# High parts of queries and keys written twice to DRAM in stack order, in a windowed attention and recurrent-gate kernel on one Trainium2 core

## What is computed

```
qkv = x @ w_in.T                       # 16 heads of 16 features
scores = q k^T / 4 + slope_h * distance, in blocks of 128 queries against their own and the previous block
o = softmax(scores) v ;  x1 = layernorm(x + o @ w_out.T)
for t in 16 "time steps" (the first axis of x1), batch 512:
    f, i = sigmoid(x1_t Wf + c Uf + bf), sigmoid(x1_t Wi + c Ui + bi);  g = tanh(x1_t Wc + c Uc + bc)
    c = f * c + i * g
h = tanh(x1 Wo + c_final Uo + bo) ;  out = layernorm(x1 + h)
```

## Time and profile before

| | |
|---|---|
| median of three runs | 1033.92 us (1031.19 to 1034.87) |
| the profiled execution | 1031.44 us, its span 1029.7 us |
| TensorE, VectorE, ScalarE busy | 914.9, 768.7, 547.5 us |
| moved by DMA | 131.98 MB, 125 GB/s of HBM traffic over the span |
| written to HBM | 50.33 MB |
| the first raw scores start at | 42.47 us |
| time of one pass in the steady part | 51.7 to 51.9 us (first raw scores of successive sequences) |

### The profile page before, as it was taken

How to read it: one execution, slowest core, us unless ns; L and a number is a source line. 1 busy time by engine, 2 the same in 40 slices (tenths; PEclk the granted TensorE clock), 3 DMA queues, 4 the chain that set the end, 5 groups by cost and what they waited for, 6 DMA issues and landing times.

```text
span 1029.7 us, 25853 instructions
## 1 busy us (share of the span) xinstructions
PE 914.9 (89%) x9500; PEld 750.3 (73%) x9500; DVE 768.7 (75%) x2882; ACT 547.5 (53%) x1101; POOL 376.7 (37%) x621
## 2 busy tenths in 40 slices
PE   3287879999999999999999999999999989889994
PEld 2164667878787878787878787878787867678884
DVE  6356767787879797979797979797979684336885
ACT  5034544555555555656565656565555544325876
POOL 3023433343434344444444444444434342201443
PEclk9578989999999999999999999999999989999998
DMA  7545353545353535353535453545354410112764
GB/s 199 143 134 140 106 166 110 155 125 151 113 156 117 151 111 156 107 157 118 152 111 151 123 148 115 153 119 150 118 131 120 125 50 23 42 53 71 215 201 137
DMA packets 92957, 131.98 MB, mean 128 GB/s; under 512 B 12008, under 2 KB 46696, under 8 KB 92832
## 3 DMA queue, kind: packets, MB, share of 16 engines
q1 hardware_dynamic: 92832, 130.34, 43.9%
HBM read 78.84 MB, written 50.33 MB: 125 GB/s over the span
## 4 chain that ended last, share of the span: by engine, by line
PE 55%; DVE 29%; ACT 5%; SPq 3%; issue 3%; POOL 2%; DMA 2%; ACTq 0%; POOLq 0%; DVEq 0%
PE bank L903 24%; DVE bank L665 12%; PE bank L957 8%; PE bank L891 7%; PE bank L922 6%; PE bank L943 3%; DVE qk_parts L638 3%; DVE y L707 3%; PE bank L965 3%; DVE max_q L665 2%; DVE cT L638 2%; PE bank L998 1%; ACT qk_parts L416 1%; SPq L263 1%; DVE gate L720 1%
## 5 line engine op out<-in xcount | busy, mean ns | idle before, releaser
L665 DVE CUSTOM_DVE_ANT_0 bank<-bank,mask 128x256 f32<-128x256 f32 (+1 forms) x1024 | 367.9, 420 | 99.9 <-PE bank L922 98.4
L433 ACT ACTIVATE Pt<-bank 128x512 f32<-128x512 f32 (+1 forms) x512 | 248.5, 536 | 217.6 <-PE bank L943 217.4
L352 POOL TENSOR_SCALAR_AFFINE_SELECT Pt<-Pt 128x512 f32<-128x512 f32 x256 | 176.9, 691 | 473.2 <-ACT Pt L433 473.2
L922 PE MATMUL bank<-Ks,Qs 58*128 58x256 f32 (+1 forms) x1024 | 150.2, 320 | 74.6 <-DVE max_q L665 49.8
L922 PEld LDWEIGHTS bank<-Ks,Qs 58*128 58x128 f32 x1024 | 108.3, 191 | 121.2 <-issue 56.9
L354 POOL TENSOR_SCALAR_AFFINE_SELECT Pt<-Pt 128x384 f32<-128x384 f32 x256 | 148.7, 581 | 0.0
L665 DVE DVE_READ_ACCUMULATOR2_ANT max_q<- 128x1 f32 x1024 | 142.2, 139 | 0.1
L957 PE MATMUL bank<-Pt,Vp 128*32 128x256 f32 (+1 forms) x2048 | 129.1, 373 | 3.1 <-POOL Pt L354 3.1
L903 PE MATMUL bank<-x1T,Wg 64*128 64x512 f32 x960 | 127.6, 397 | 0.0
L903 PE MATMUL bank<-cT,Ug 64*128 64x512 f32 x960 | 125.6, 393 | 0.0
L943 PE MATMUL bank<-Qs,Ks 59*128 59x256 f32 (+1 forms) x1024 | 112.0, 271 | 1.9 <-DMA Qs<-max_rows 1.3
(11 more groups left out here) (109 smaller groups left out, 1334.6 us busy)
## 6 DMA issues: line engine op xcount, KB each, us to landing
parts_dram<-qk_parts SPq DMA_DIRECT2D x128, 256.0 KB
Qs<-parts_dram SPq DMA_DIRECT2D x128, 128.0 KB, 2.6
Ks<-parts_dram SPq DMA_DIRECT2D x128, 128.0 KB, 2.7
xt_raw<-in_xt SPq DMA_DIRECT2D x16, 512.0 KB, 4.2
Qs<-parts_dram SPq DMA_DIRECT2D x128, 64.0 KB, 2.7
Ks<-parts_dram SPq DMA_DIRECT2D x128, 64.0 KB, 2.7
x_res<-in_x SPq DMA_DIRECT2D x16, 512.0 KB, 3.9
x_dram<-y SPq DMA_DIRECT2D x16, 512.0 KB, 3.0
```

The lines of the kernel that those rows point to most:

```text
L352: gp.affine_select(out=p4[:, :, 0:128], in_=p4[:, :, 0:128], compare_op=ALU.is_ge, fill=0.0, base=0, pattern=[[0, 4], [1, 128]], channel_m ...
L433: sc.activation(probabilities(g, 2 * pair + odd)[:, S * a:S * a + n], SC[odd][:, 0:n], ACT.Exp).then_inc(exp_done, 1)
L665: ins = ve.tensor_tensor_reduce(out=raw, in0=raw, in1=mask[:, keys], scale=1.0, scalar=MASKED, op0=ALU.add, op1=ALU.max, accum_out=max_q[: ...
L922: ins = te.matmul(MX[odd][:, 256 * (n % 2):256 * (n % 2) + 256][:, keys], Qs[rows, 2 * g + pair, n * WIN:(n + 1) * WIN], Ks[rows, 2 * g + ...
```

## The change

The DRAM buffer gets three parts per head rather than two, in the order of the stack: high, low, high for queries and high, high, low for keys. parts_to_dram writes three transfers of 256 KB for queries and three for keys, so the high part goes out twice. A refill then reads 48 neighbouring rows in one transfer, for queries and keys, even and odd heads: four per call. The waits for parts_out go from 32 to 48 per sequence, in `stack` and in `qk_hi`. The order of SP's work, and everything on the other engines, stays.

```diff
-ROWS_Q = ((0, 0, 2), (2 * D, 0, 1))
-ROWS_K = ((0, 0, 1), (D, 0, 2))
+THIRDS_Q = (0, 1, 0)
+THIRDS_K = (0, 0, 1)
...
-STACK_DMAS = 8
+STACK_DMAS = 4
...
-        parts_dram = nc.dram_tensor("parts_dram", [2, 2, 2, H // 2, 2, D, S], F32).ap()
+        parts_dram = nc.dram_tensor("parts_dram", [2, 2, 2, H // 2, 3, D, S], F32).ap()
...
-                    for part in range(2):
-                        sp.dma_start(parts_dram[t % 2, c, which, :, part, :, :],
+                    for n, part in enumerate((THIRDS_Q, THIRDS_K)[which]):
+                        sp.dma_start(parts_dram[t % 2, c, which, :, n, :, :],
                                      qk_parts[:, c, which, part, :].bitcast(F32)).then_inc(parts_out[c][which], 16)
...
-                    wait(sp, parts_out[c][which], 32, t, 32)
-                for which, (dst, groups) in enumerate(((Qs, ROWS_Q), (Ks, ROWS_K))):
+                    wait(sp, parts_out[c][which], 48, t, 48)
+                for which, dst in enumerate((Qs, Ks)):
                     src = parts_dram[t % 2, c, which].rearrange("(b o) l d s -> o (l d) b s", o=2)
                     for odd in range(2):
-                        for r, part, n in groups:
-                            sp.dma_start(dst[64 * odd + r:64 * odd + r + n * D, 2 * g:2 * g + 2, :].bitcast(F32),
-                                         src[odd, part * D:(part + n) * D, b:b + 2, :]).then_inc(stacked[g], 16)
+                        sp.dma_start(dst[64 * odd:64 * odd + 3 * D, 2 * g:2 * g + 2, :].bitcast(F32),
+                                     src[odd, :, b:b + 2, :]).then_inc(stacked[g], 16)
...
-                wait(act, parts_out[k // 2][k % 2], 32, t - 1, 32)
+                wait(act, parts_out[k // 2][k % 2], 48, t - 1, 48)
```

## The result

The changed kernel takes 1042.93 us (median of 10 runs, 1040.65 to 1047.47), the kernel before, beside it, 1034.22 us. The ratio is 1.0083, with a 95% interval of 1.006 to 1.0105: slower by 8.7 us, inside the range, on the side that was forecast as the likelier, and 3.1 us more than the sum said. The profiled executions differ by more, 1042.41 against 1031.44 us, 11.0 us.

What follows compares the result with a forecast made beforehand. SP and DMAs were taken to matter until about 130 us, then PE and DVE; 4.6 + 0.3 + 0.4 + 0.3 = 5.6 us on 1031.44 gave 1037.0 us, or 1039.5 against the median; range 1034.5 to 1045.0 us.

Steps and rivals of the forecast that it cites:

- the three signs: Forecast wrong if steady score matmuls wait for max_rows, the pass changes length, or first raw scores miss 45 to 49 us.
- The two regimes: Until about 130 us SP and DMAs are on the path; after, PE and DVE set passes of 51.7 to 51.9 us.
- The cost of a write: Each added 256 KB write drains in 1.34 us, on half the DMA engines at 195 GB/s.
- The start: Sequence 0, before first raw scores: four added writes delay group 0's last refill by 4.6 us, bounds 3.0 and 6.4.
- Sequence 0, group 0 of sequence 1: Scores waiting for the maxima behind these refills: 2.7 us later landing, less 0.5 and 1.9 us, +0.3 us.
- Sequence 1: Two terms: its second half, refills of group 1, +0.4 us; group 0 of sequence 2, +0.3 us.
- The saving of the refills: SP's queue: a 48-row issue takes 0.46 us, four take 2.0 us, so a group saves 1.9 us (0 to 3.0).
- The steady passes: Maxima of group 2 land 0.8 us later, hidden by slack of 2.2 to 3.9 us: 0 us.
- rival (c): Steady part: maxima of group 2 over 3.5 us later, TensorE waits in every pass; 1051 us, chance 0.09.
- (b): Added writes spread over all 16 engines: 2.7 us at the start, +1.0 us in all, 1035 us; chance 0.08.
- (d): Faster: fewer refill issues shorten three places of the fill, added writes overlap waits; 1031 us or less, chance 0.05.
- (a): Start mostly hidden: landing follows issue, +3.0 us, about 0 at the other three places; 1036 to 1037 us, chance 0.20.

Runs made afterwards that it cites:

- the writes alone: The changed kernel with refills cut back to 32 and 16 rows, eight per group: 1049.72 us, ratio 1.0131 against the kernel before.
- the one with the maxima ahead: The changed kernel with the maxima of group 2 sent before the refills of the next sequence's group 0: 1042.37 us, ratio 1.0074 against the kernel before.
- the change in the fill only: Sequences 0 to 2 with three writes and 48-row refills, later ones as in the kernel before: 1042.05 us, ratio 1.0068.
- the change after the fill: The changed kernel, but sequences 0 to 2 keep two writes and eight refills: 1038.31 us, ratio 1.0036 against the kernel before.
- the other layout: The changed kernel with the three rows of one feature side by side in DRAM, so writes spread over 16 engines: 1027.74 us, ratio 0.9913.
- the big refills alone: The kernel before (two writes) with four 48-row refills that read on into the next rows, some products wrong: 1032.36 us, ratio 0.9958.
- the fastest kernel: The kernel before (two writes, eight refills) with feature-major DRAM layout, keys stored low, high: 1024.33 us, ratio 0.9881.

## Why the prediction was right, and where it was off

**The number** is inside the range, in part by luck. Two of the three signs that I had named for a wrong forecast came: score matmuls wait for max_rows in the steady part, and passes change their length (four of them take 52.2 to 53.0 us). The range took that up because it had room above the sum, meant for a larger start and the spread of the median. Against the profiled execution, from which it was summed, the 5.6 us were 11.0.

**The two regimes** hold in the main. TensorE and VectorE still set most passes; but the border isn't at 130 us, since a transfer exceeds its slack in four later passes too.

**The cost of a write.** 1.34 us each at half of the DMA share: the same share and rate appear again in the changed kernel, the writes alone cost 5.4 us at the start, and spreading the same bytes over all engines turns 0.8% slower into 0.9% faster. This is shown.

**The start.** Said +4.6 us, with 3.0 and 6.4 as bounds; it was +3.3 in the trace of the changed kernel. Two more kernels have the same program up to there, the one with the maxima ahead and the one with the change in the fill only: their first raw scores start at 46.5 and 47.1 us, +4.0 and +4.6, and their last refills of group 0 land 6.00 and 6.73 us after issue, beside the 5.88 us above. Two kernels that begin like the one before start at 42.2 and 42.9 us, beside its 42.5. So executions differ here by 1.3 us, and the term holds.

Beside the writes alone (+5.4) the big refills give 0.8 to 2.1 us back. I had written that their saved issue gives nothing where the drain sets the end.

**Sequence 0, group 0 of sequence 1:** said +0.3, was +1.0. From the first write's issue to the maxima's landing it takes 1.1 us more (16.9 us, 15.9 before). The second DMA of the maxima lands 3.11 us after its issue, not 1.78 us, which I hadn't allowed for.

**Sequence 1** (the next two terms): said +0.7 together, was +3.6, with the steady passes the largest miss. It has two parts. From the issue of the writes for sequence 2 to the landing of the maxima it takes 17.7 us, 15.7 before: +2.0 where I said +0.3. The writes take 2.6 us more, the issues up to the maxima 1.9 us less, and the maxima land 3.13 us after issue rather than the 1.79 us of the earlier trace rows, 1.3 us more. This repeats: 17.5 us with the change in the fill only, 15.7 us where it begins after the fill.

```profile
132.47 3.13 DMA Qs<-max_rows
```

The other 1.6 us come before those writes go out, where I said +0.4. A raw score matmul waits 1.1 us for the refills of group 1 there, and TensorE's clock is at half speed for 15.5 us of the pass, 10.7 us before. How much each is worth isn't settled: the kernel that is like the one before up to there has 23.9 us of half speed in that pass and takes 4.2 us longer in the same part without the change.

**The saving of the refills.** The size was right, 0.43 us per 48-row issue and some 1.9 us per group. What failed is the step from issue to landing. I took it that the maxima, issued 1.9 us earlier, land 1.8 us after their issue. They queue behind four refills that SP now sends about twice as fast; with the same writes and eight smaller refills (the writes alone) they land 1.8 us after issue in nine of the twelve steady passes, here after 2.6 to 3.9 us. From the landing of the writes to the landing of the maxima it takes 6.6 us in the kernel before and 6.5 us in the changed one, on average over sequences 3 to 14; with two writes and big refills it is 6.5 us in the pass at 480 us, there because the maxima aren't ready. So in the steady part the saved 1.9 us bring 0.1 us; in sequence 0 they brought 2.0 us, in sequence 1 0.6 us.

**The steady passes.** Said 0 us, because 0.8 us would be taken from a slack of 2.2 to 3.9 us. The writes take 3.1 us more from first issue to landing on average (11.7 us, 8.6 before), less the 0.1 us: the maxima come 3.0 us later, 2.0 to 4.1 us from pass to pass. In four of the twelve passes that is more than the slack, and they cost 3.5 us in the profiled execution, 0.36% on the median of the kernel with the change after the fill. That is rival (c) at its edge, with the place right (the maxima of group 2) and the price a third: I asked for lateness of more than 3.5 us in every pass, and four have it. It isn't the passes with the smallest slack that pay: sequence 7 had 2.2 us and lost 2.1 us of it, sequence 12 had 3.6 us and its maxima came 3.9 us later. In three of the four that pay (6, 11 and 13) the writes took 12.8 to 13.0 us, in all others 11.1 to 11.5 us; why wasn't tested.

**The other rivals.** (b) would have had the share of the added writes at 1; it was 0.52, and only the other layout has 1.01. The figure that (b) takes from the Trainium skill (DMA: Bandwidth & Descriptors, "Anatomy of one DMA"), 436 GB/s, is given there for transfers issued by GpSimd; here SP issues them, and the other layout moved 365 GB/s. The Trainium skill's rule to coalesce small transfers (DMA: Bandwidth & Descriptors, "Rules for kernel authors") is borne out by the big refills alone, at 0.4%, and outweighed here by the writes that they need. (d) fell with the ratio. (a) said 45.5 us for the start, and three traces have 45.8, 46.5 and 47.1 us; it was wrong on what follows.

**What was said to show it:** first raw scores at 47 us (45.8 to 47.1); a 48-row issue under 0.5 us (0.43); 148.8 MB and 67 MB (148.74 and 67.11); SP's wait for the writes near 4 us per pass (it was 4.3):

```profile
SPq L174 <- DMA parts_dram<-qk_parts: 64.5, 15, 5.6
```

## What to carry to other kernels

Before trading transfers for bytes, read the DMA share while only that transfer runs: at 0.5, as here, look at the shape of its DRAM side before the count of issues; one rearrangement gained 1.2% with no byte more or less. An issue saved on the queue is only worth what lands earlier: follow it to the landing of the last small DMA behind it. And don't set a usual lateness against a usual slack: here both differ by about 2 us between passes, and the few passes where lateness is the larger pay. Last, before a difference of a few us in one trace is given to a cause, look at what another trace of the same program part has.

## What the runs showed of the hardware that was not expected

In the fill TensorE's granted clock falls back to half several times, and not at the same times in each trace. The half-speed stretches that begin between 40 and 200 us add up to 23.9 us in the trace of the kernel before, 30.7 in the changed one and 41.0 in the kernel that equals the one before until sequence 3 (from the clock records; 1.0 of the granted clock in all steady stretches). A few us gained or lost in the fill can so be enlarged or hidden; the fastest kernel starts 7.1 us earlier than the one before, has 34.1 us of half speed, and is 6.0 us ahead at its end in the profiled execution, 12.5 us by the medians. The times of one and the same kernel go with it: of 29 executions of the kernel before, the nine with a mean granted clock of 0.955 to 0.957 took 1031.1 to 1032.8 us, and the six with 0.946 or 0.947 took 1036.4 to 1039.9 us. What makes the clock fall was not tested.
